# The order of key and value projections for attention 2, between attention 1 and the Mamba-2 block

## The reference, cut to what matters

```
# block 0: attention of x over the context, 16 heads of 16, with a mask per query and key
Q, K, V = x @ Wq.T + bq, ctx @ Wk.T + bk, ctx @ Wv.T + bv
a = softmax(where(mask == 0, -1e9, Q K.T / 4)) V
x = layernorm(a @ Wo.T + bo + x) * ln_g + ln_b
# block 1: a Mamba-2 block on x, then attention over the same context, 8 heads of 32
zxbcdt = rms(x) @ in_proj_w            # gate z, channels x/B/C, steps dt
xBC = silu(causal depthwise conv of 4 taps);  dt = softplus(dt + bias)
y = state-space scan over the 512 positions (8 heads x 64, state 128)
x = x + rms(y * silu(z)) @ out_proj_w
k, v = ctx @ Wk1, ctx @ Wv1            # the projections that the change reorders
x = x + softmax(ln(x) @ Wq1 k.T / sqrt(32)) v @ Wo1
```

## Time and profile before

| | us |
|---|---|
| median of 3 runs | 8695.27 (8695.15 to 8697.0) |
| the profiled execution, its own time | 8695.25 |
| its span, first to last instruction | 8693.3 |
| TensorE busy / VectorE / ScalarE / GpSimd | 7601.7 / 4991.8 / 3399.7 / 1907.4 |
| mean granted TensorE clock | 0.927 of full speed |

### The profile page before, as it was taken

How to read it: one execution, slowest core, us unless ns; L and a number is a source line. 1 busy time by engine, 2 the same in 40 slices (tenths; PEclk the granted TensorE clock), 3 DMA queues, 4 the chain that set the end, 5 groups by cost and what they waited for, 6 DMA issues and landing times.

```text
span 8693.3 us, 128104 instructions
## 1 busy us (share of the span) xinstructions
PE 7601.7 (87%) x37572; PEld 3396.5 (39%) x37572; DVE 4991.8 (57%) x12397; ACT 3399.7 (39%) x4278; POOL 1907.4 (22%) x1864
## 2 busy tenths in 40 slices
PE   3989889898998989889898898989989899898988
PEld 0343433434334343433434334343343433434343
DVE  3566465664656556465664656646566564656646
ACT  0424435243352434435244352433524335252443
POOL 3040130402203031130401304023030311303113
PEclk6989999899998989989899898999989999898998
DMA  3142240423314132131422304233141331314223
GB/s 72 26 79 37 39 69 10 79 37 50 57 21 75 30 61 55 21 69 27 76 40 36 67 14 79 37 47 60 20 76 30 56 58 19 71 30 71 45 36 61
DMA packets 216827, 422.15 MB, mean 49 GB/s; under 512 B 35673, under 2 KB 126715, under 8 KB 215945
## 3 DMA queue, kind: packets, MB, share of 16 engines
q1 hardware_dynamic: 214103, 413.20, 27.9%
q10 hardware_dynamic: 2048, 0.53, 0.0%
HBM read 191.17 MB, written 8.54 MB: 23 GB/s over the span
## 4 chain that ended last, share of the span: by engine, by line
PE 69%; DVE 11%; issue 8%; DMA 6%; ACT 3%; POOL 1%; SPq 1%; DVEq 0%; ACTq 0%; POOLq 0%
PE ps L1029 14%; PE ps L966 11%; PE ps L1000 8%; PE ps L1002 8%; PE ps L928 7%; DVE mx L1635 6%; PE ps L1004 4%; DMA kst<-khl 4%; PE ps L1034 4%; PE ps L1148 2%; PE ps L985 2%; PE ps L1239 1%; DMA qst<-q1hl 1%; PE ps L1267 1%; ACT PR L1406 1%
## 5 line engine op out<-in xcount | busy, mean ns | idle before, releaser
L1406 ACT ACTIVATE PR<-ps 128x1024 f32<-128x1024 f32 x2496 | 2499.6, 1024 | 2505.0 <-PE ps L1002 1494.4
L1606 DVE CUSTOM_DVE_ANT_0 ps<-ps,maskq 128x402 f32<-128x402 f32 x4203 | 2409.0, 587 | 1505.6 <-PE ps L966 1362.7
L1029 PE MATMUL ps<-PR,vbuf 128*32 128x512 f32 x9984 | 1343.3, 610 | 5.1 <-ACT PR L1406 5.1
L1002 PE MATMUL ps<-maskk,identb 128*128 128x512 bf16 x3328 | 1263.4, 380 | 0.0
L966 PE MATMUL ps<-kst,qst 96*128 96x402 bf16 (+1 forms) x3115 | 1019.5, 340 | 79.5 <-DVE mx L1606 64.3
L1635 DVE TENSOR_REDUCE mx<-ps 128x2 f32<-128x804 f32 x1024 | 932.6, 987 | 167.8 <-PE ps L985 164.9
L985 PE MATMUL ps<-kst,qst 100*128 100x402 f32 x2048 | 744.2, 488 | 257.8 <-DMA qst<-q1hl 155.4
L1000 PE MATMUL ps<-qst,kst 99*128 99x512 bf16 x2496 | 950.7, 381 | 0.0
L1004 PE MATMUL ps<-qst,kst 102*128 102x512 f32 x1664 | 767.9, 525 | 100.2 <-ACT PR L1406 70.8
L966 PEld LDWEIGHTS ps<-kst,qst 96*128 96x128 bf16 x3115 | 281.8, 97 | 1182.3 <-DVE mx L1606 821.3
L746 POOL MEMSET kst<- 96x252 f32 (+1 forms) x34 | 8.7, 255 | 3063.1 <-PE ps L1029 3016.6
(11 more groups left out here) (197 smaller groups left out, 7669.8 us busy)
## 6 DMA issues: line engine op xcount, KB each, us to landing
kst<-khl SPq DMA_DIRECT2D x96, 800.5 KB, 16.1
kst<-khl SPq DMA_DIRECT2D x300, 200.1 KB, 7.4
stage<-in_maskt SPq DMA_DIRECT2D x204, 256.0 KB
stage<-in_mask SPq DMA_DIRECT2D x204, 201.0 KB
ctxs<-in_ctxt SPq DMA_DIRECT2D x17, 1601.0 KB, 25.8
qst<-q1hl SPq DMA_DIRECT2D x96, 256.0 KB
win_s<-in_w_in SPq DMA_DIRECT2D x16, 1288.0 KB, 5.7
KS<-khl SPq DMA_DIRECT2D x102, 200.1 KB
```

The lines of the kernel that those rows point to most:

```text
L1002: mm = pe.matmul(o, identb[:, :], maskk[:, t, :], start=False, stop=True)
L1029: mm = pe.matmul(ps[32 * j:32 * j + 32, 6, :], l, PR[:, t % 2, j, :], start=(t == 0), stop=(t == KT - 1), tile_position=(0, 32 * j))
L1406: nc.scalar.activation(PR[:, t % 2, 2 * half:2 * half + 2, :], ps[:, 2 * half:2 * half + 2, :], ACT.Exp, scale=scale).then_inc(s_p, 1)
L1606: nc.vector.tensor_tensor_reduce(src, src, maskq[:, i, c0:c0 + w], 1.0, -3.0e38, ALU.add, ALU.max, mx[:, c, h * QT + i:h * QT + i + 1]).th ...
```

## The change

SECOND begins with the four pieces of key block 0; value tiles 0 to 9 follow, then key block 1 and value tiles 10 to 12. So the eight items behind the output projection are the four pieces and value tiles 0 to 3, and steps 0 to 2 of the input projection are followed by value tiles 4 to 6 in place of three key pieces; from step 3 on the items are the same as before. TensorE and ScalarE both take the order from the list. On GpSimd the four subtractions (`parts` of K1[:NC]) move ahead of the wait for the layer norm's moments. The stack copies keep their three DMAs and their conditions.

```diff
--- before.py
+++ after.py
@@ -377,7 +377,7 @@
                 FRONT, BACK, V0 = q + k[0], k[1], v
                 PJ += FRONT + BACK + V0
             else:
-                SECOND, LASTQ = v[:V_LN] + k[0] + v[V_LN:KT - 3] + k[1] + v[KT - 3:], q
+                SECOND, LASTQ = k[0] + v[:KT - 3] + k[1] + v[KT - 3:], q
                 PJ += SECOND + LASTQ
         pj_index = {item: n for n, item in enumerate(PJ)}
 
@@ -780,6 +780,9 @@
                 alone(pool)
                 clear_k1(b, 1, GH // 2)
 
+                for item in K1[:NC]:
+                    parts(b, item)
+
                 pool.wait_ge(s_mom, QT * (b + 1))
                 alone(pool)
                 nc.gpsimd.tensor_scalar(rstd[:, 0, :], moments[:, :, 1], EPS, 1.0, ALU.add, ALU.mult).then_inc(s_ve, 1)
@@ -798,9 +801,6 @@
                     pool.wait_ge(s_rm, n)
                     nc.gpsimd.tensor_tensor(rstd[:, 1, cols2], rstd[:, 1, cols2], neghalf[:, cols2], ALU.pow)\
                         .then_inc(s_rms, 1)
-                for item in K1[:NC]:
-                    parts(b, item)
-
                 def spread_a(c):
 
                     pool.wait_ge(s_a, b + 1)
```

## The result

The changed kernel takes 8626.57 us (8620.68 to 8630.34, median of 4 runs), the kernel before 8695.21; the ratio is 0.992, with a 95% interval of 0.9907 to 0.9934. It is faster by 69 us, not by the 157 that were forecast, and its time lies outside the range of 8508 to 8575. The profiled execution took 8623.85 us.

The account below looks back on a forecast made before the run. TensorE, busy 87%, was taken to stall each pass on a late stack copy and GpSimd's aU. Terms -13.0 + 4.6 - 1.5 + 0.1 = -9.8 us per pass, 16 passes, -157 us: 8538 us, range 8508 to 8575.

Parts of the forecast that it names:

- The stall: TensorE's 10.44 us standstill before the fourth window sums goes; with the half-speed items after it, -13.0 us per pass.
- the slow clock: Two TensorE items after the standstill, 5.97 us at reduced clock, return to 3.44; 2.5 us gained per pass.
- The layer norm's delay: First rstd comes 5.35 us later behind four GpSimd subtractions; transposes and input projection start later, +4.6 us per pass.
- the handshake: ScalarE and GpSimd take turns on single buffer `rest`, ahead of rstd; one key piece per 1.74 us.
- The shorter fill: Value tiles replace k1, k2, k3 in the input projection's first three places; -1.5 us per pass.
- The shared port: VectorE and GpSimd exclude each other in SBUF, first to start winning; sum stays 8538 if GpSimd starts first.
- Rival 2: VectorE's line 1702 holds up GpSimd's subtractions, layer norm 1.5 us later still; 8562 us, chance 0.07.
- Rival 1: Clock or fourth aU helps less than thought, 1 to 3 us per pass; about 8570 us, chance 0.10.

Follow-up runs that it names:

- The interleaved kernel: Changed kernel with key pieces and value tiles alternating behind the output projection, and GpSimd's four subtractions spread around the layer norm's steps; 8515.7 us.
- the reciprocal: Kernel before, with one more 128x128 reciprocal on VectorE per pass ahead of the layer norm's last scaling; 8751.51 us.
- its pause filled: Changed kernel with ten extra 128x512 matmuls per pass on TensorE, results unread, in its wait ahead of the row maxima; 8540.43 us.

## Why the prediction was right and where it was wrong

**The stall** went as predicted, with the slow clock behind it: -10.3 and -2.4 against -10.3 and -2.5. The copies had the time that was worked out for them.

**The layer norm's delay** was right in mechanism and size: the four subtractions start at 959.18, 960.90, 962.73 and 964.45, so the three rounds between them took 1.72, 1.83 and 1.72 us against 1.74, and rstd came 5.30 later against 5.35. The subtractions took 0.89 to 1.15 us; the prediction read the earlier ones as 1.03 to 1.34 and missed one of 0.90 at 984.49, which made no difference to the sum. The interleaved kernel, which takes the handshake away from ahead of rstd, gets 4.5 us a pass back.

**The shorter fill** was mis-sized, -0.4 in place of -1.5. The premise that failed is "If the clock again returns 7.05 us after 981.6": it returned at 983.6, 9.2 us behind the start of line 1179 (974.38), and the first 512-column projection took 3.62 us in place of 2.28. The windows of the changed kernel, on both sides of the return:

```profile
974.38:983.50 9.12, 9.12 (x26) 6.61 (x26) 3.58 (x18) 1.90 (x7) 0.94 (x1) 0.50 1.04 112
983.70:986.00 2.30, 2.30 (x9) 1.27 (x8) 1.35 (x2) 1.16 (x3) 0.76 (x1) 1.00 1.06 121
```

The half clock had begun earlier, by the clock record at 969.9 in the pause of 3.76 us ahead of the transposes (before at 973.8, between the transposes): it lasted 13.7 us now and 10.2 us before. This is the same error as below, on a small scale: a time of the clock was carried over as if it were fixed to the work.

**The shared port.** Rival 2 did not come about: VectorE's four scalings at 959.98 stretched to 2.35 us (1.67 before) and the first three subtractions took 1.04 to 1.15. Nearly the whole stretch lies in the fourth scaling: it started 0.3 us behind the second subtraction and took 1.12 us, the other three 0.47 to 0.52. GpSimd won there, at a place where VectorE had 4.45 us to spare. That agrees with the rule quoted in the prediction, in the case in which GpSimd starts first. The second subtraction itself started 0.1 us behind VectorE's third scaling and took 0.1 us longer than the first, where rival 2 had 1.5 us a pass.

**What was wrong** is the sentence "Everything behind the scan's start is released by events of this stretch ..., so it keeps its distances and moves with it." What fails is "keeps its distances". The releases did move along, as line 985's wait for q1hl and the steady idle times show, but the stages behind do not run at one clock, and the same matmuls took longer there. The sum had no term for it, and the range none either. It cost 5.0 us a pass, 81 of the 157 us: 3.7 in the row maxima, 0.6 and 1.3 in the attentions, less 0.6 ahead of the row maxima; the other 8 or so are the 0.3 a pass between 9.8 and 9.5 and the scatter of the runs. Rival 1 had the clock in it, with 1 to 3 us a pass, but placed it in the stretch ahead of the scan alone, and had a chance of 0.10. The windows of the kernel before had the sign: a clock of 0.77 in the row maxima is a stage at neither of the two levels throughout, so its length rests on when the clock falls and rises. That every pass read 0.77 and 529 us looked like a property of the work, and was one of its place in time. There was a second sign: VectorE is busy 59.3 of the 62.2 us there, so the stage had little to gain from its place and several us to lose.

The Trainium skill, "TensorE: Matmul & The Clock Gate", section "What's actually happening", says that what decides the clock watches on its own, free-running, and does not restart with the kernel, so that the same kernel may rise at another point from run to run. The trace agrees in that the kernel shifted once by 1.7 us takes 64.8 and 64.2 us for a stage that otherwise takes 62.2. Of the rise at a kernel's start the page adds that the cost is under 1% of a typical span and not to be fitted. Here the clock falls and rises again in every pass; what it took is 81 of 8695 us, 0.9% of the time, but more than half of the gain that was forecast.

**Left open.** Why the kernel before holds itself at its favourable place, and the changed one doesn't, was not tried. What the runs show is that a held place belongs to no one kernel and need not be a good one: 529 us a pass for the kernel before, 532.5 with the reciprocal, 518.5 to 519.0 for the changed kernel with its pause filled, 525.5 to 525.8 for seven passes of the changed kernel shifted once. Nor was it tried which instruction of the row maxima brings the clock down. And each kernel has one profiled execution, so how a pass of it varies from launch to launch is not shown.

## What to carry to other kernels

Before summing a saving inside a loop, look at the granted clock of every stage behind it, not only of the stage that changes. A stage between the two levels is a place where a saving can be lost, or more gained than was worked for, so the range should include that stage at its shortest and longest. Tell a real gain from a lucky place with a control: shift the kernel by a microsecond once ahead of the loop and by one per pass, and compare the stages, not the totals. And when work is moved ahead of a short scalar step that others wait for, put it behind that step in pieces, each where its input is ready: that was worth 72 us here, on top of the change's own 69; the 39 us beyond came from the clock and can't be counted on.

## What the runs showed of the hardware that was not expected

A launch of 8.7 ms became 55 us longer for 15 us of work spread over the passes; another did not get longer at all with the same 15 us added. Two matmuls of 1.7 us in all, once ahead of the loop, made the first two passes 5.7 and 2.7 us longer and left the third as it was. In all kernels the busy time of VectorE in the row maxima stays at 59.2 to 59.6 us and TensorE's idle time at 8.1 to 9.6 us, while TensorE's granted clock moves between 0.70 and 0.80 and its busy time with it.
